# Two graph attention layers: layer 1 shifted by the top of the first eighth of the rows, its opening work moved into layer 0 and its own first eighth, output halves stored by two queues, one block of programs

## The reference

```python
h = jnp.maximum(_layernorm(x, axis=-1), 0.0)
x = x + _L0_gnn_ref(h, L0_gnn_W, L0_gnn_a, adj, 8192)
h = jnp.maximum(_layernorm(x, axis=-1), 0.0)
x = x + _L1_gnn_ref(h, adj, L1_gnn_W, L1_gnn_a)
```

```python
e = jax.nn.leaky_relu(e_src[:, None] + e_dst[None, :], negative_slope=ALPHA)
attention = jax.nn.softmax(jnp.where(adj > 0, e, NEG_INF), axis=1)
h_prime = attention @ Wh
```

## Time and profile before

| what | value |
|---|---|
| median of 3 runs | 2001.0 us (1999.59 to 2002.02) |
| the profiled execution: its time | 2002.71 us |
| its span, first to last instruction | 2000.9 us (1.8 us lie around it) |
| busy: PE, DVE, ACT, POOL | 1914.1, 1750.4, 1453.3, 1255.5 us |
| mean granted TensorE clock | 0.981 |
| read from DRAM, written | 548.54 MB, 16.32 MB; 282 GB/s over the span |

### The profile page before, as it was taken

One profiled execution on the slowest core, in us unless ns is written; L12 is line 12 of the kernel. 1 busy time (PEld: TensorE's weight loads), 2 busy tenths in 40 slices (PEclk: granted clock), 3 DMA queues, 4 the chain that ended last, 5 costly groups with the idle time before them and its releaser, 6 DMA issues.

```text
span 2000.9 us, 39030 instructions
## 1 busy us (share of the span) xinstructions
PE 1914.1 (96%) x16858; PEld 1902.6 (95%) x16858; DVE 1750.4 (87%) x2026; ACT 1453.3 (73%) x1677; POOL 1255.5 (63%) x1010
## 2 busy tenths in 40 slices
PE   4789999999999999999968999999999999999997
PEld 3689999999999999999967999999999999999997
DVE  7888898989989898998957998898989899898985
ACT  4988788969888798888820767777777777778700
POOL 3675766767777676767720556767777776768600
PEclk9799999999999999999988999999999999999999
DMA  8998897999989898897982777888988888889900
GB/s 247 350 339 340 287 334 245 335 335 317 317 287 320 275 321 304 280 320 272 325 283 96 269 295 275 293 311 293 337 276 325 283 296 309 294 315 306 316 10 13
DMA packets 182339, 567.49 MB, mean 284 GB/s; under 512 B 18704, under 2 KB 50832, under 8 KB 180752
## 3 DMA queue, kind: packets, MB, share of 16 engines
q0 software_dynamic: 142848, 520.16, 74.4%
q1 hardware_dynamic: 34960, 42.67, 6.4%
q10 hardware_dynamic: 4352, 2.10, 0.5%
HBM read 548.54 MB, written 16.32 MB: 282 GB/s over the span
## 4 chain that ended last, share of the span: by engine, by line
PE 89%; DVE 6%; DMA 2%; ACT 1%; POOL 1%; issue 0%; SPq 0%; DVEq 0%; POOLq 0%
PE psum L659 87%; PE psum L632 1%; DMA arena<-in_adj_dram,piece_rows 1%; DVE arena L906 1%; DVE arena L740 1%; DVE arena L891 1%; ACT arena L343 1%; DVE arena L884 1%; PE psum L621 0%; DMA arena<-in_x_dram 0%; DVE st L715 0%; POOL piece_rows L379 0%; PE psum L599 0%; DVE arena L361 0%; DVE h_all L761 0%
## 5 line engine op out<-in xcount | busy, mean ns | idle before, releaser
L659 PE MATMUL psum<-h_all,arena 128*128 128x129 f32 x16384 | 1842.4, 276 | 10.4 <-DVE arena L906 10.4
L659 PEld LDWEIGHTS psum<-h_all,arena 128*128 128x128 f32 x16384 | 1837.9, 192 | 14.0 <-DVE arena L906 9.2
L333 POOL DMA_INDIRECT arena<-in_adj_dram,piece_rows x992 | 1246.1, 1256 | 641.4 <-ACT arena L343 446.1
L343 ACT ACTIVATE arena<-arena,half_step 128x1024 uint8<-128x1024 int32 x992 | 1365.1, 1437 | 313.1 <-DVE arena L361 161.3
L906 DVE SCALAR_TENSOR_TENSOR arena<-arena,rho_col 128x1024 f32<-128x1024 f32 x896 | 1125.8, 1277 | 169.1 <-PE psum L659 165.0
L361 DVE STREAM_TRANSPOSE arena<-arena 128x1024 f32<-128x1024 f32 x248 | 305.9, 1234 | 9.1 <-ACT arena L343 9.1
L906 DVE SCALAR_TENSOR_TENSOR arena<-psum,rho_col,arena 128x1024 f32<-128x1024 f32 x128 | 158.7, 1267 | 17.7 <-PE psum L659 14.6
L343 ACT ACTIVATION_READ_ACCUMULATOR arena<-arena,half_step 128x1 f32 x512 | 91.0, 178 | 0.0
L632 PE MATMUL psum<-W_ext,arena 128*128 128x131 f32 x256 | 40.5, 324 | 13.8 <-DVE h_all L761 10.7
L632 PEld LDWEIGHTS psum<-W_ext,arena 128*128 128x128 f32 x256 | 38.1, 234 | 15.4 <-issue 8.1
L621 PE MATMUL psum<-ident,arena 128*128 128x128 f32 x128 | 20.0, 308 | 32.9 <-DVE arena L740 32.5
(11 more groups left out here) (111 smaller groups left out, 180.9 us busy)
## 6 DMA issues: line engine op xcount, KB each, us to landing
arena<-in_adj_dram,piece_rows POOLq DMA_INDIRECT x992, 5.9
arena<-in_x_dram SPq DMA_DIRECT2D x48, 128.0 KB, 6.2
x_mid<-arena SPq DMA_DIRECT2D x8, 512.0 KB, 5.5
edgesT<-arena SPq DMA_DIRECT2D x4, 1024.0 KB, 8.9
arena<-edgesT SPq DMA_DIRECT2D x4, 1024.0 KB, 11.1
arena<-r_mid SPq DMA_DIRECT2D x1, 4096.0 KB, 12.0
arena<-x_mid SPq DMA_DIRECT2D x8, 512.0 KB, 6.8
out_dram<-arena SPq DMA_DIRECT2D x32, 128.0 KB, 9.8
```

The source lines that it names most:

```text
L333: pool.indirect_dma_start(adj_in[n % NA], None, adj_pieces, bass.IndirectOffsetOnAxis(ap=piece_rows[:, column:column + 1], axis=0))\
L343: nc.scalar.activation(pack_bytes[h][:, k, a], adj_in[n % NA], ACT.Sign, bias=half_step[:, 0:1], accum_out=into).then_inc(masked, 1)
L659: last = nc.tensor.matmul(acc_tile(g, k), wTs[m % RING][:, k * P:(k + 1) * P], h_all[:, j, 0:FZ], start=(j == 0 and k % 2 == 0), stop=(j = ...
```

## The change

- **Shift.** The shift of layer 1 is `ref`, the largest e_dst of the first 1024 rows. It is found in eighth 2 of layer 0 (`find_reference`), so the exponentials of layer 1 can be taken eighth by eighth: `keep_h` multiplies D into h while it copies it out (eight small activations for two large ones) and takes rho and r of its eighth (`next_exps`). r is cut at a limit (`limit_r`), and the verdict checks that `top` is at most 20 above `ref`.
- **Loads.** In layer 0's last eighth SP loads h back part by part behind the sums that still use the old one (`load_h1`), stores and spreads r of six eighths (3 MB), and loads the kept edges one by one. The seventh eighth of h is written into `h_all` directly.
- **The last eighth of layer 0** is finished inside layer 1's first one, at the tiles of `last_at` (DVE) and at PE's tiles 26 and 30, ACT's pieces 6 and 9 of pass 17. Only tile 56 needs it. The judgement and the last r values are placed behind tile 36.
- **Means.** They are added to the residual at tile 61 (`add_means`), ahead of the end of the sums, with a mask from the neighbour counts.
- **The end.** The last eighth is stored in two halves, two blocks of each by SP and two by ACT (`store_last`).
- **Blocks.** The engines read the verdict at the end of their fast programs, SP and ACT before their last stores, and branch inside the same block (`general_if`).

```diff
+            def next_exps(t0, t1):
+                d, c = sd_next[:, t0:t1, 1], slice(t0, t1)
+                nc.scalar.activation(rho_next[:, c], d, ACT.Exp, scale=1.0 - ALPHA, bias=exp_bias[:, 1:2])
+                nc.scalar.activation(r_next[:, c], sd_next[:, t0:t1, 0], ACT.Exp, scale=ALPHA - 1.0, bias=exp_bias[:, 1:2])\
+                    .then_inc(next_ready, 1)
...
+            def load_h1(i):
+                if i == 0:
+                    sp.wait_ge(h1_stored, 16 * READY)
+                sp.wait_ge(summed, (NG - 1) * T + (i + 1) * TP)
+                sp.dma_start(h_all[:, part_of(1, i), 0:F], h1_mid[i].rearrange("p (t f) -> p t f", f=F))\
+                    .then_inc(first_loaded if i == 0 else h1_loaded, 16)
...
+            load_h1(0)
+            load_h1(1)
+            store_r(1, 0, READY * TP)
+            load_r(2, slice(0, READY * GW))
+            load_h1(2)
+            load_h1(3)
+            sp.wait_ge(edges_stored, 16 * SUBS)
+            load_kept(0)
+            store_x(NG - 2)
+            load_h1(4)
+            load_kept(1)
+            load_h1(5)
+            load_kept(2)
+            load_xr(NG - 1)
+            load_kept(3)
...
-            store_out(NG - 1)
-            sp.wait_ge(out_stored, 16 * BK * NG)
+            flagged = read_path(sp)
+            for half in range(2):
+                store_last(sp, half, 0)
+            sp.wait_ge(out_stored, 16 * BK * (NG + 1))
+            return flagged
...
                 for half in range(2):
-                    act.wait_ge(h_done[1], 2 * i + half + 1)
-                    ps = h_ps(1, i, half)
-                    nc.scalar.activation(sd_next[:, half_of(i, half), :], ps[:, :, F:F + 3], ACT.Identity)\
-                        .then_inc(sd_kept, 1)
...
+                    keep_sd(i, half)
+                    if i == READY:
+                        act.wait_ge(summed, (NG - 1) * T + (READY + 1) * TP)
+                    act.wait_ge(D_next_ready, 2 * i + half - 1)
+                    for t in range(half * TP // 2, (half + 1) * TP // 2):
+                        b = i * TP + t
+                        into = tiles(ye)[:, t, :] if i < READY else h_all[:, b, 0:F]
+                        last = nc.scalar.activation(into, h_ps(1, i, half)[:, t - half * TP // 2, 0:F], ACT.Identity,
+                                                    scale=D_next[:, b:b + 1])
+                    last.then_inc(h_kept[1], 1)
+                act.wait_ge(sd_kept, 2 * (i + 1))
+                next_exps(0 if i == 1 else i * TP, (i + 1) * TP)
...
+            act.wait_ge(summed, (NG - 1) * T + (NG - 1) * TP)
+            set_D(0, (NG - 1) * TP)
             elu(NG - 1)
-            warm_up(2, ACT.Sqrt)
             deviation(1, NG - 1, part_of(1, NG - 1))
-            warm_up(3, ACT.Exp)
-            keep_zT(NG - 1)
-            keep_h(NG - 1)
-            exps(1)
             for n in range((NG * COLS + 1) * PIECES, len(PASSES) * PIECES):
+                if n == (NG * COLS + 1) * PIECES + 6:
+                    keep_zT(NG - 1)
+                if n == (NG * COLS + 1) * PIECES + 9:
+                    keep_h(NG - 1)
+                    set_D((NG - 1) * TP, T)
                 mask_piece(act, n)
...
+                    if layer == 1 and g == 0 and j == (NG - 1) * TP:
+                        pe.wait_ge(h_kept[1], 2 * NG)
+                        pe.wait_ge(D_set, 2)
...
+            last_at = {5: 0, 7: 1, 9: 2, 12: 3, 13: 4, 14: 5, 20: 6, 21: 7, 22: 8}
+            reference_at = {12: 0, 19: 1, 26: 2}
...
+                    if j == 61:
+                        add_means(g)
```

More of the change, by code:

```diff
@@ L70 @@
 FOLDS = 8
+READY = NG - 2
 CB = CH // P
@@ L400, in load_x, with read_path, store_last @@
                 eng.dma_start(x_all[q, part_of(0, i), :], block).then_inc(x_loaded[i], 16)
+        def read_path(eng):
+            eng.wait_ge(path_ready, 1)
+            return eng.value_load(path[0:1, 0:1], min_val=0, max_val=1)
+        def store_last(eng, half, which):
+            eng.wait_ge(half_ready, half + 1)
+            mine = slice(half * TP // 2, (half + 1) * TP // 2)
+            for q, block in quarters(out, ORDER[NG - 1])[2 * which:2 * which + 2]:
+                eng.dma_start(block[:, mine, :], tiles(xo)[q, mine]).then_inc(out_stored, 16)
         def sync_fast(sp):
@@ L450, in sync_fast @@
             load_r(1, slice(3 * GW, N))
-            for g in range(1, NG):
+            for g in range(1, NG - 1):
                 store_x(g - 1)
@@ new lines, in keep_first_h @@
+            def keep_first_h():
+                act.wait_ge(x_stored, 16)
+                for half in range(2):
+                    keep_sd(0, half)
+                    into = tiles(ye)[:, half * TP // 2:(half + 1) * TP // 2, :]
+                    nc.scalar.activation(into, h_ps(1, 0, half)[:, :, 0:F], ACT.Identity).then_inc(h_kept[1], 1)
+            def keep_h(i):
+                if i == 1:
+                    act.wait_ge(ref_ready, 1)
+                    act.wait_ge(sd_kept, 2)
+                    nc.scalar.activation(D_next[:, part_of(1, 0)], sd_next[:, part_of(1, 0), 1], ACT.Exp, scale=ALPHA,
+                                         bias=exp_bias[:, 0:1])
+                if i < READY:
```

417 lines of the change are left out of this document (245 added, 172 removed).

## The result

| | median | runs | range |
|---|---|---|---|
| before | 2000.3 us | 4 | 1998.11 to 2002.02 |
| changed | 1974.15 us | 4 | 1969.02 to 1978.42 |

The ratio is 0.987, with a 95% interval of 0.9847 to 0.9892: 26 us faster. The four runs of the changed kernel lie at 1969.0, 1970.1, 1978.2 and 1978.4 us, further apart than those of before. The profiled execution is the fastest of them, 1969.02 us, with a span of 1967.1.

What follows compares the result with a forecast made beforehand. TensorE's sums were taken as the bound; 34.2 - 2.7 - 0.6 - 2.3 - 0.5 - 5.0 + 1.5 + 5.2 = 29.8 us saved, so 2001.0 - 29.8 = 1971.2 us; 8-in-10 range 1963 to 1979 us.

Steps and rivals of the forecast that it cites:

- the stall: PE's wait at `products(1, 6)` in layer 0's last eighth: 5 us taken, 0 to 12 possible; 2 to 8 given 0.47.
- The boundary: Between the layers: 32.1 us and 2.1 us of slow sums removed, 34.2 together; PE idle under 1 us there.
- Layer 0's last eighth: Added loads crowd the DMA engines, pieces come 16 us late, 11 are free, `keep_zT(6)` delays the products: 5.0 us lost.
- no collision: Rival: added loads in layer 0's last eighth cause no stall, 5 us stay: 1966 us; chance 0.30.
- my own sign: Prediction is wrong if, in layer 0's last eighth, PE's products do not wait for ACT (L553).
- Layer 1's first eighth: Slow sums -2.1, moved transposes and products +2.7, small transposes and spreads +0.6, waits for DVE +2.3, residual load +0.5 us.
- the crowd: DVE's extra work at tiles 46 to 62 of layer 1's first eighth makes PE wait 1.0 us.
- the rival of a residual that comes 4 us late: Part of the larger-collision rival: late residual costs 3.5 us at the means, 12 at the products; 1982 us, chance 0.19.
- Layer 1's other eighths: PE's gap of 0.23 us per eighth closes: 7 x 0.2 = 1.5 us gained.
- The end: From last sum to kernel end: 14.1 us becomes 8.9, a gain of 5.2 us (3.5 to 6).
- the slower rival: Sums without rest between layers drop TensorE to 1.2 GHz in layer 1; 70 us of it gives 2006 us; chance 0.02.
- the general path: Rival: the fast path is not taken and the whole general path follows, more than 2000 us; chance 0.01.

Runs made afterwards that it cites:

- the second set: Later group of runs on an undisturbed chip, in which the changed kernel was measured once more, unaltered (e8_again2): 1975.55 us.
- e11_general: The kernel with the verdict's reach limit set to -100, so the general path always runs; 9903.86 us in one run.
- e4_res_early: Changed kernel with the residual for the first means loaded ahead of the last store and load of r; 2125.66 us, ratio 0.9547, disturbed chip.
- e9_order: Changed kernel with ACT's square root, `keep_zT(6)` and `keep_h(6)` moved ahead of late pieces in layer 0's last eighth; 2128.74 us, ratio 0.9598, disturbed chip.
- e5_all: Changed kernel with 2.5 MB of r loaded later, the square root before piece 12 and the residual loaded earlier; 1967.98 us, ratio 0.9831.
- e7_old_end: Changed kernel with the end of the kernel before (one store, verdict read in its own block), means still ahead; 1978.46 us, ratio 0.9883.
- e8_again2: The changed kernel measured once more, unaltered, on an undisturbed chip; 1975.55 us, ratio 0.9873.
- e12_r_late2: Changed kernel with only 2.5 MB of r loaded later, behind the kept edges, a repeat on another, disturbed chip; 2130.08 us, ratio 0.9682.
- e10_best: Changed kernel with the edits of e9_order and e5_all together; 2143.45 us, ratio 0.9598, disturbed chip.

## Why the prediction was right, point by point

The prediction was 1971.2 us, between 1963 and 1979; measured was 1974.15, and 1975.55 in the second set. That the sum came within 3 us of the median is in part luck: the first four runs stood near 1969.5 and near 1978.3, on both sides of it, and 5 us for the stall is near none of the waits seen. By its own steps, against the table of stretches:

- **The boundary** (32.1 us gone, no wait left on PE): as predicted.
- **Layer 0's last eighth** (5.0 us predicted, 0 to 12 as bounds): that late pieces hold up `keep_zT` and through it the products was right; one number could not hold it. Layer 0 grew by 3.6 us in one execution and by 11.5 in another. Of the 3.6, 0.6 is the eighth in which the reference is searched (118.5 us for 117.9), 1.8 the waits of the sums for DVE (below), 0.7 what comes with them (a tile behind a wait takes 2.06 us instead of 1.79, last section) and 0.2 the wait of the products; the other 0.3 are small pieces of PE. Of the 11.5, 6.5 is the wait of the products, 1.9 their work at the lower clock level, 0.6 the sums behind them, 2.1 the waits of the sums and what comes with them, 0.6 the reference. Over all profiles with ACT's and r's order as changed here, the products waited 0.2, 6.5, 7.0, 9.1, 9.6, 6.3 (e11_general) and 7.2 us (e4_res_early, with the residual early): the typical wait lies above my 5, and the changed kernel never showed the 1966 us of the rival "no collision". `keep_zT` came 14.3 us later than before in the one execution and 19.8 in the other (from ACT's arrival at 1002.0 us, each counted from the start of its steady sums); 16 were estimated, and 11 are free (PE came to the products 3.2 and 2.3 us later itself, so 0.2 and 6.5 us became a wait). So the size of the delay was met. But it was worked out from the rate of the DMA engines alone, and in the slower execution a gather issue of 8.48 us lies in it; and the term has nothing for the lower clock behind the stall. By my own sign, "wrong if the products do not wait", the first profile, with its 0.2 us, nearly spoke against me.
- **What I did not name:** the square root. The first late step is not `keep_zT` but L540, which DVE wants between two tiles. DVE and PE in the timeline of the changed kernel:

```profile
995.13 0.20 DVE L854 RECIPROCAL rstd<-std 128x8 f32<-128x8 f32 x1 [5.27 <-ACT std L540]
...
997.51 2.05 PE L766 MATMUL psum<-h_all,arena 128*128 128x129 f32 x16 [1.42 <-DVE arena L1063]
999.74 2.05 PE L766 MATMUL psum<-h_all,arena 128*128 128x129 f32 x16 [0.17 <-DVE arena L1063]
1001.96 5.62 PE L766 MATMUL psum<-h_all,arena 128*128 128x129 f32 x48 [0.17 <-DVE arena L1063]
```

  The pieces are late, so the square root behind them is, so DVE stands for 5.27 us with a tile to form behind it, its four tiles of lead are spent, and PE waits 1.42 us and two times 0.17. In e9_order, with the root six pieces earlier, DVE has no such wait. Behind this wait DVE also catches up in one run of seven tiles, the run in which six other profiles show a held issue of POOL.
- **Layer 1's first eighth** (predicted -2.1 + 2.7 + 0.6 + 2.3 + 0.5 = +4.0 us): +3.8. The size was right, its parts less so. PE in the timeline of the changed kernel:

```profile
1075.42 2.05 PE L766 MATMUL psum<-h_all,arena 128*128 128x129 f32 x16 [0.17 <-DVE arena L1063]
...
1083.48 2.05 PE L766 MATMUL psum<-h_all,arena 128*128 128x129 f32 x16 [0.22 <-DVE arena L1063]
...
1153.04 17.13 PE L766 MATMUL psum<-h_all,arena 128*128 128x129 f32 x150 [1.14 <-DVE arena L1063]
```

  Around tiles 20 to 26 the sums waited 0.56 us in three short waits (1.3 predicted); near tile 62 there is one of 1.14 us (1.0 for the crowd and 0.5 for the residual were predicted). The residual itself was almost in time, as DVE's row of `add_means` in the same timeline shows:

```profile
1148.35 2.19 DVE L1033 SCALAR_TENSOR_TENSOR arena<-mean_row,lin,arena 128x128 f32<-128x128 f32 x8 [0.28 <-DMA arena<-x_mid]
```

  So the 1.14 us is mostly DVE's crowd. With the residual loaded earlier (e5_all) it is 0.77, but e7_old_end, which loads it late, has 0.76: the rival of a residual that comes 4 us late fell, and the early load shows no gain. Some 1.0 us more comes with the four waits (0.27 us each beyond what is recorded, last section), which I did not count.
- **Layer 1's other eighths** (-1.5): -2.9. The gaps are gone (7 x 0.23 = 1.6, PE busy for 801.10 of 801.10 us), and as much again, which I did not count: before, from the tile behind one gap to the tile behind the next took 114.84 us; now 7200 matmuls run in 804.4 us, which is 114.40 for an eighth. Each gap cost 0.44 us, of which the profile shows 0.23 as a wait.
- **The end** (14.1 to 8.9, gain 5.2): 14.1 to 9.7, gain 4.4. The issues of the changed kernel's end in its timeline, and the rows of lines L428 and L1790 (engine, op, ns min/median/max, first and last start):

```profile
1957.48 0.17 DVE L1039 TENSOR_SCALAR inv<-psum 128x8 f32<-128x8 f32 x1 [4.82 <-PE psum L766]
...
1959.08 3.48 SPq L428 DMA_DIRECT2D out_dram<-arena  x4
1959.08 3.48 ACTq L428 DMA_DIRECT2D out_dram<-arena  x4
```

```profile
L428 SPq DMA_DIRECT2D out_dram<-arena x4: 323/488/1862, 1959.1 to 1960.7; - x4
...
L1790 PEldq COMPARE_BRANCH  x1: 3571/3571/3571, 1956.2 to 1956.2; - x1
...
L1790 SPq COMPARE_BRANCH  x1: 45/45/45, 1964.3 to 1964.3; - x1
```

  With T = 1957.4 the first issue starts at T + 1.7 (1.5 predicted) and the fourth at T + 3.3 (3.0). SP goes on to its branch at T + 6.9 where I had the landing at T + 5.3: the mis-sized term is the last issue, which took 1.86 us where four issues took 1.84 together before. From the branch to the end are 2.8 us (3.6 predicted). By the experiments the means ahead bring 2.6 us of the gain and halves, two queues and the early verdict some 1.7.
- **TensorE's clock** over layer 1 is 1.00 without the rest between the layers: the slower rival did not happen, nor did the general path.

The Trainium skill (DMA: Bandwidth & Descriptors, "Issuing engines are not separate DMA queues"), on which the prediction drew, says that transfers interleave on the same 16 DMA engines whoever issues them, and that several issuing engines save issue time only. The traces agree at both places: SP's loads and the gathers of POOL together stand at a share of 1.02, and what two queues saved at the end, 1.4 us, is of the size of issue time, since eight issues by SP alone took 5.49 us and four on each queue 3.48.

So of the 32.1 us between the layers, 4.4 at the end and 2.9 in the late eighths, 3.8 are given back in layer 1's first eighth and 3.6 or 11.5 in layer 0, which leaves the 32.0 and 23.9 us of the table. That the levels near 1970 and 1978 us in the unprofiled runs are this wait, present or absent, is what the two profiles suggest; those runs have no trace, so it is argued and not shown.

## What to carry to other kernels

When a transfer moves into a busy stretch, don't ask only whether the stretch has room: find the engine whose input comes late and read what stands behind that input in its program. Work that another engine waits for should stand ahead of pieces that nobody needs yet; in e9_order that took three changed lines and no transfer, and the wait was gone. When a piece is late, look also at the engine that issues it: in each of the six longest stops here, one issue of POOL had taken nine times its usual time. And bring in early only what is wanted first: of the 3 MB of r, 0.5 were needed for the next eighth.

## What the runs showed of the hardware

- A pause of TensorE costs more than itself. Windows of e8_again2 in the wait of the products, in the products, and in the sums behind them (the granted clock is the third number from the right):

```profile
1011.80:1018.30 6.50, 0.04 (x2) 0.01 (x1) 1.28 (x1) 4.90 (x5) 4.20 (x5) 0.86 1.03 389
1018.30:1022.00 3.70, 3.70 (x17) 3.70 (x18) 0.00 (x0) 3.30 (x3) 1.71 (x3) 0.50 1.02 407
1022.00:1026.00 4.00, 4.00 (x32) 4.00 (x32) 1.28 (x1) 2.26 (x4) 1.55 (x2) 0.84 1.03 409
```

  After 6.46 us without work the products ran at 0.50, the lower level (1.2 GHz), for 3.86 us instead of the 1.95 of e9_order. 3.7 to 3.9 us stand behind all waits of 5.7 to 9.6 us; behind 2.66 us it was 2.95, and behind 2.11 us 2.06. The 512 sums behind took 58.35 us, and 57.71 in the execution of 1969.0. So the stop of 6.46 us cost 9.0.
- Even a short wait of TensorE costs more than the profile shows as a wait. The tile that began at 997.51 us was followed by the next at 999.74, 2.23 us later, with 0.17 us of wait between them; without a wait a tile takes 1.79. So 0.27 us more go with each.
- One issue of a gather by POOL, 0.95 us in the median, took 8.1 to 9.2 us in six profiles, each time during a run of seven tiles on DVE and until 0.8 us behind it; in a seventh profile the same run held none. In runs of three to five tiles (e9_order, e12_r_late2, e10_best) it was 4.3 to 5.5 us. The cause stays open.
- The DMA engines moved 375 to 409 GB/s with gathers and plain loads side by side, at shares of 1.01 to 1.03, in windows of 3.7 to 69 us.
- Four issues in a row took 0.32, about 0.49 (the median) and in the end 1.86 us when SP and ACT issued at the same time; of eight by SP alone the longest was 1.71 us.
- The branch over the general path's program is recorded with 3.57 us on PE's queue, but PE meets it beside its last sums, at 1956.2 us, so it no longer stands behind the stores.
